# Scatters of the dense edges in node order, 108 of 508 of them and 75 dense blocks ahead of the first layer's pairs, and the gathers without their wait for dense progress

## What is computed

```python
def genconv(x, src, dst, W1, b1, g, be, W2, b2):          # three layers of the first network
    msg = relu(x[src]) + 1e-7
    m = segment_max(msg, dst)
    ex = exp(msg - m[dst])
    alpha = ex / segment_sum(ex, dst)[dst]
    out = segment_sum(msg * alpha, dst) + x               # per node: a softmax-weighted mean of its edges
    h = out @ W1 + b1
    h = relu((h - h.mean(0)) * rsqrt(h.var(0) + 1e-5) * g + be)
    return h @ W2 + b2

def layer(x, ea, src, dst, nw, ew, fnw, fnb, few, feb):   # three layers of the second network
    h, e = relu(x @ nw.T), relu(ea @ ew.T)
    n2 = relu(concat([segment_sum(e, dst), h]) @ fnw.T + fnb)
    e2 = relu(concat([h[src] + h[dst], e]) @ few.T + feb)
    return n2, e2

h = relu(layernorm(x)); x = x + three_genconv(h)          # relu behind each of the three
h = relu(layernorm(x)); x = x + three_layers(h, edge_attr)
```

## Time and profile before

| | |
|---|---|
| median of three runs | 4170.22 us (4170.03 to 4172.24) |
| the profiled execution | 4165.19 us, of which the span of the core is 4163.4 |
| mean granted clock of PE | 0.894 of full speed |
| PE busy | 3299.3 us, 79% |
| POOL busy | 2373.3 us, 57% |
| DVE busy | 2217.1 us, 53% |
| ACT busy | 1941.5 us, 47% |
| setup | 0 to about 863 us |
| first gather and last gather of layer 0 | 863.46 and 1391.62 us |

### The profile page before, as it was taken

How to read it: one execution, slowest core, us unless ns; L and a number is a source line. 1 busy time by engine, 2 the same in 40 slices (tenths; PEclk the granted TensorE clock), 3 DMA queues, 4 the chain that set the end, 5 groups by cost and what they waited for, 6 DMA issues and landing times.

```text
span 4163.4 us, 70803 instructions
## 1 busy us (share of the span) xinstructions
PE 3299.3 (79%) x19961; PEld 2595.9 (62%) x19961; DVE 2217.1 (53%) x5689; ACT 1941.5 (47%) x3697; POOL 2373.3 (57%) x2488
## 2 busy tenths in 40 slices
PE   2287777769898789888699888758788888888887
PEld 0144444458777677777577777746666666666665
DVE  6144333325444555445665445736666666666666
ACT  0222111146555576555585555734444444444444
POOL 2666666646666366666356665255565565565552
PEclk6588988889999899999899999879999999998988
DMA  7155433467777367777367776554444444444442
GB/s 291 54 184 191 138 119 120 124 202 246 248 235 236 117 231 234 251 234 242 110 230 243 243 235 197 151 160 126 124 129 129 127 128 128 128 125 127 127 125 63
DMA packets 419116, 713.14 MB, mean 171 GB/s; under 512 B 75585, under 2 KB 259067, under 8 KB 416098
## 3 DMA queue, kind: packets, MB, share of 16 engines
q0 software_dynamic: 130688, 321.08, 26.0%
q1 hardware_dynamic: 270119, 323.45, 25.5%
q10 hardware_dynamic: 18107, 66.24, 4.2%
HBM read 561.11 MB, written 149.39 MB: 171 GB/s over the span
## 4 chain that ended last, share of the span: by engine, by line
PE 36%; another core or an unknown queue 18%; issue 14%; DVE 14%; ACT 10%; DVEq 2%; ACTq 2%; DMA 1%; SPq 1%; POOL 0%; POOLq 0%
PE ps L1570 17%; PE ps L1593 4%; ACT casts L1466 2%; PE ps L718 2%; DVE acc L2369 2%; DVE acc L2403 2%; PE ps L2242 2%; DVE onehot L2396 1%; PE ps L2221 1%; ACTq L934 1%; DVE acc L2396 1%; PE ps L712 1%; ACT two_parts L1456 1%; PE ps L700 1%
## 5 line engine op out<-in xcount | busy, mean ns | idle before, releaser
L2211 POOL DMA_INDIRECT ring<-h_table,idx_ring x832 | 815.9, 981 | 563.2 <-issue 272.9
L652 POOL DMA_INDIRECT pair_rings<-split_table,src_idx x728 | 713.6, 980 | 409.8 <-issue 202.5
L1570 PE MATMUL ps<-casts,two_parts 128*128 128x500 f32 (+1 forms) x3464 | 823.1, 391 | 141.4 <-DVE two_parts L1660 73.8
L1570 PEld LDWEIGHTS ps<-casts,two_parts 128*128 128x128 f32 x3464 | 646.3, 198 | 280.2 <-DVE two_parts L1660 83.5
L665 POOL DMA_INDIRECT adjacency<-acc x508 | 495.8, 976 | 344.4 <-issue 144.7
L1660 DVE TENSOR_TENSOR two_parts<-work,two_parts 128x512 fp32r<-128x512 f32 (+1 forms) x276 | 187.4, 679 | 588.9 <-ACT two_parts L1456 349.8
L1466 ACT ACTIVATE casts<-spare 128x1000 fp32r<-128x1000 fp8e4 (+1 forms) x471 | 458.9, 974 | 8.5 <-PE ps L1570 4.8
L2308 ACT ACTIVATE work<-acc,vecs 128x512 f32<-128x512 f32 x208 | 150.2, 722 | 562.4 <-DVE acc L2369 303.5
L1456 ACT ACTIVATE two_parts<-work 128x512 fp32r<-128x512 f32 (+1 forms) x276 | 169.7, 615 | 452.8 <-remote 232.5
L2221 PE MATMUL ps<-ident,ring 128*128 128x128 f32 x1664 | 292.3, 298 | 83.6 <-issue 59.2
L2260 PEld LDWEIGHTS ps<-mats,work 128*128 128x128 f32 x1664 | 238.2, 204 | 141.7 <-issue 140.4
(11 more groups left out here) (333 smaller groups left out, 6242.6 us busy)
## 6 DMA issues: line engine op xcount, KB each, us to landing
spare<-adjacency SPq DMA_DIRECT2D x216, 250.0 KB
acc<-e_few SPq DMA_DIRECT2D x208, 256.0 KB
work<-msg_table SPq DMA_DIRECT2D x144, 256.0 KB
work<-in_edge_attr SPq DMA_DIRECT2D x104, 256.0 KB
e_few<-spare SPq DMA_DIRECT2D x52, 512.0 KB
spare<-rel_rows SPq DMA_DIRECT2D x208, 84.0 KB
spare<-adjacency SPq DMA_DIRECT2D x72, 187.5 KB
e_few<-work SPq DMA_DIRECT2D x26, 512.0 KB
```

Of the source, the lines that this page charges most:

```text
L652: e.indirect_dma_start(out=to, out_offset=None, in_=table, in_offset=bass.IndirectOffsetOnAxis(ap=src_idx[:, 2 * i + h, j:j + 1], axis=0)) ...
L1570: ins = e.matmul(bank, parts_of(d)[:, b % 2, q, kind * D:(kind + 1) * D], cast_counts[n % CASTS][:, at:at + width], start=opens, stop=(b = ...
L2211: e.indirect_dma_start(out=rows[:, s, j, :], out_offset=None, in_=h_table, in_offset=bass.IndirectOffsetOnAxis(ap=idx_ring[:, s, j:j + 1], ...
```

## The change

- **Order of the columns.** The 508 columns become 4 segments (SEGMENTS) of 127 (WIDE): row p of segment s holds 127 edges, and the segments lie behind one another in the order of destinations. Scatters 0 to 126 so fill the lowest destinations and 381 to 507 the highest. Each comparison on DVE covers 4 x (127 + k) columns instead of 508 + k, and a few small operations are added.
- **Clearing.** Regions 0 and 1 are cleared first; then x is loaded; then regions 2 and 3 are cleared. Scatter 0 waits for the first two regions alone, scatter 127 for the rest.
- **Where the scatters stand.** 400 (EARLY) stay in the setup, with their wait for the attributes; the last 108 stand on POOL at the head of the edges phase of layer 0, without that wait, ahead of the first gather. SP waits for all of them before it loads the first counts of region 2. The places and the counts get tiles of their own.
- **Dense blocks of layer 0.** 75 (LEAD_BLOCKS) stand in 15 steps ahead of the first pair, 5 in each; the other 121 are spread evenly over the 42 steps. Layers 1 and 2 keep their order.
- **Gathers.** The wait at h == 1 for `dense` is gone in all three layers; the wait for the sum of pair i-3 stays.

```diff
+SEGMENTS = 4
+WIDE = COLS // SEGMENTS
+REACH = WIDE + 2 * NEAR
+EARLY = 400
+LEAD = 15
+LEAD_BLOCKS = 75
...
-def step_of(n):
+def step_of(layer, n):
     r, b = divmod(n, BLOCKS)
+    columns = [sum(widths) for _, widths in REGIONS]
+    before = sum(BLOCKS * w for w in columns[0:r]) + b * columns[r]
+    if layer == 0:
+        lead = sum(columns[k // BLOCKS] for k in range(LEAD_BLOCKS))
+        if n < LEAD_BLOCKS:
+            return n * LEAD // LEAD_BLOCKS - LEAD
+        return (before - lead) * PAIRS // (BLOCKS * sum(columns) - lead)
...
             for h in range(2):
-                if h == 1:
-                    reached(e, S("dense"), blocks_halfway(i - 1))
...
-        def scatters(e, S):
-            e.wait_ge(S("zero_fill"), 16 * FILLS * len(REGIONS))
-            e.wait_ge(S("addresses"), 1)
-            for i in range(COLS):
+        def scatters(e, S, first, end):
+            for i in range(first, end):
                 n = i // EACH
+                if i == 0:
+                    e.wait_ge(S("zero_fill"), 16 * FILLS * 2)
+                if i == WIDE:
+                    e.wait_ge(S("zero_fill_rest"), 16 * (FILLS * (len(REGIONS) - 2) + 1))
                 if i % EACH == 0 and n >= SCATTERS:
                     e.wait_ge(S(f"gather_spread{n % SCATTERS}"), 16 * EACH * (n // SCATTERS))
-                if i % EACH == 0:
+                if i % EACH == 0 and i < EARLY:
                     reached(e, S("few_e0"), 2 * pairs_behind(n))
...
-                e.tensor_tensor(same[k % 4][:, 0:n], key[:, NEAR - k:NEAR + COLS], key[:, NEAR:NEAR + n], ALU.is_equal).then_inc(S("hit"), 1)
+                e.tensor_tensor(same[k % 4][:, :, 0:n], key[:, :, NEAR - k:NEAR + WIDE], key[:, :, NEAR:NEAR + n], ALU.is_equal).then_inc(S("hit"), 1)
...
-                scatters(e, S)
-                scattered(e, S)
+                e.wait_ge(S("addresses"), 1)
+                scatters(e, S, 0, EARLY)
+                scattered(e, S, EARLY)
                 split_stored0(e, S)
...
+                    for r in range(2):
+                        clear(r)
                 for k in range(5):
...
+                if not again:
+                    for r in range(2, len(REGIONS)):
+                        clear(r)
...
+                    if ready and d == 2 * DUOS:
+                        scattered(e, S, COLS)
...
             def pool(e, S):
+                if ready:
+                    scatters(e, S, EARLY, COLS)
                 for i in range(PAIRS):
                     reached(e, S("sums"), free_after(i))
...
-                for i in range(PAIRS + 3):
-                    blocks = [n for n in range(ALL_BLOCKS) if step_of(n) == i]
+                for i in range(-lead, PAIRS + 3):
+                    blocks = [n for n in range(ALL_BLOCKS) if step_of(layer, n) == i]
```

More of the change, by code:

```diff
@@ L83, in chunks_before @@
     return sum(len(widths) for _, widths in REGIONS[0:r])
-def step_of(n):
+def step_of(layer, n):
     r, b = divmod(n, BLOCKS)
+    columns = [sum(widths) for _, widths in REGIONS]
[5 more added lines that the diff above has]
+        return (before - lead) * PAIRS // (BLOCKS * sum(columns) - lead)
     if r == 0:
         return b * FIRST_STEPS // BLOCKS
[L91 to L99, removed]
+    first = BLOCKS * columns[0]
+    return FIRST_STEPS + (before - first) * (PAIRS - FIRST_STEPS) // (BLOCKS * sum(columns) - first)
 def slot_of(i):
@@ L140, in dense_jobs @@
             for n in range(width // CH):
-                jobs.append((step_of(BLOCKS * (r + 1) - 1) + 3, CUT + at + n * CH, chunks, False))
+                jobs.append((step_of(layer, BLOCKS * (r + 1) - 1) + 3, CUT + at + n * CH, chunks, False))
             at += width
-    out, now = [], -1
+    out, now = [], -LEAD - 1
     for ready, node, least, sparse in sorted(jobs):
@@ L922, in act, with clear @@
             def act(e, S):
+                def clear(r):
+                    width = PITCH if sum(REGIONS[r][1]) > PITCH // 8 * 7 else sum(REGIONS[r][1])
+                    rows = adjacency[r * SPAN * PITCH:r * SPAN * PITCH + NR * PITCH, :].rearrange("(p b d) o -> p b (d o)", b=BLOCKS, d=PITCH)
+                    for h in range(FILLS):
+                        at = slice(h * BLOCKS // FILLS, (h + 1) * BLOCKS // FILLS)
+                        n = at.stop - at.start
+                        zeros = Z0[:, 0:-(-n * width // 4)].bitcast(U8)[:, 0:n * width].rearrange("p (b d) -> p b d", d=width)
+                        e.dma_start(rows[:, at, 0:width], zeros).then_inc(S("zero_fill" if r < 2 else "zero_fill_rest"), 16)
                 if not again:
@@ L1295, in edges_phase @@
             columns = iota_w[:, :]
+            lead = LEAD if ready else 0
+            JOBS = JOBS_OF[layer]
             by_node = [work[0:WW, b, 0:2 * D] for b in range(2)]
@@ L1341, in duos_at @@
             def duos_at(i):
-                return [d for d in range(ALL_DUOS) if step_of(first_block(d)) == i + 1]
+                return [d for d in range(ALL_DUOS) if step_of(layer, first_block(d)) == i + 1]
             def blocks_of(u):
@@ L1355, in evacuated @@
             def evacuated(i):
[L1357 removed]
+                return [r for r in range(len(REGIONS)) if step_of(layer, BLOCKS * (r + 1) - 1) + 1 == i]
             def jobs_of(i):
@@ L1724, in dve @@
                     e.memset(hot_r[:, :, :, WW:P].bitcast(F32), 0.0).then_inc(S("blank"), 1)
-                for i in range(-1, PAIRS + 3):
+                for i in range(-lead - 1, PAIRS + 3):
                     if len(REGIONS) - 1 in evacuated(i):
```

102 lines of the change are left out of this document (51 added, 51 removed).

## The result

The changed kernel takes 4354.09 us (median of four runs, 4348.84 to 4369.62), the kernel before 4171.23 beside it: a ratio of 1.043 (95% interval 1.037 to 1.048), 183 us slower. The forecast was 4295 us with 4335 as its upper end. The direction was right, the size too small by 59 us. The profiled execution took 4348.84 us, its span 4347.1.

What follows compares the result with a forecast made beforehand. Limits differed by stage: scatters slowed the setup's loop, POOL and PE together set layer 0's pairs. Span 4163.4 + 125 (setup's 63 already taken off, layers 1 and 2 at 0) = 4288, median 4295 us; range 4150 to 4335.

Steps and rivals of the forecast that it cites:

- Start of the setup: Clearing half the table first lets scatter 0 start at 55 instead of 73.80: -18 us, bounds -12 and -20.
- End of the setup: Attributes' pairs speed up once 108 scatters leave: four at 6.10, 26 at 4.35, 137.5 instead of 182.9, -45 us.
- The crawl in the lead: Layer 0's head: unbroken indirect DMAs slow other engines to an instruction per 0.7 us or slower; PE does 15 blocks.
- until 967: Layer 0's head: POOL's 166 us stream ends at 967; PE then runs freely, 123 us to the first sum.
- Pairs of layer 0: Layer 0's pairs: 38 distances at 11.0 us, 418 us; the last gather starts at 1517.
- I take 11.0, between 10.3 and 11.7: Distance between layer 0's pairs, 11.66 before, POOL's least 10.0; the ends mean -27 and +27 us.
- The removed wait: Dropping the half-way wait in layers 1 and 2 was put at 0, with -88 and +15 kept.
- I take 0: Layers 1 and 2: no net gain, as longer streams bring the crawl; -88 if all pauses went, +15 otherwise.
- left as it was: What stands behind layer 0's last gather was assumed unchanged.
- the sign of the free lead: Layer 0's pair distance at which the freely overlapping lead turns from gain to loss, given as 10.4 us.
- The rival of a free lead: Layer 0's head: PE does 78 blocks beside POOL's stream, first sum at 981, median 4187; chance 0.22.

Runs made afterwards that it cites:

- e1: Changed kernel plus waits: every fourth of the 108 scatters heading layer 0 waits for PE's dense blocks to keep step; 4276.75 us, ratio 1.025.
- e11: Changed kernel with the last 108 scatters left out and 216 POOL fills in their place; 4238.5 us in one run.
- e17: Changed kernel where each 8th of the 108 scatters heading layer 0 waits until the last four have landed; 4252.11 us in one run, with the crawl.
- e16: Changed kernel itself, on a chip without the crawl; 3517.76 us against 3570.94 for the kernel before, ratio 0.985.
- e5: Kernel before with only node-order columns and two-part clearing, all 508 scatters in the setup, chip without the crawl; 3554.71 us, ratio 0.994.
- e4: Changed kernel with the gathers' wait for dense progress put back in all three layers; 4314.5 us, ratio 1.033.
- e18: Kernel before without the gathers' wait for dense progress, on a chip with the crawl; 4187.01 us, ratio 1.0023.
- e8: Changed kernel where each pair's third gather waits for the previous pair's gathers to land, chip without the crawl; 3591.31 us, ratio 1.006.
- e2: Changed kernel with all 508 scatters in the setup, the lead of dense blocks kept; 4282.89 us, ratio 1.026.
- e6: Kernel before without the gathers' wait for dense progress, on a chip without the crawl; ratio 0.9984.

## Why the prediction was right or wrong

**Start of the setup: right.** -18 forecast, first scatter at 55; it was 53.35, and the first store came 16.8 us earlier (187.16).

**End of the setup: right in kind, a little short.** 30 pairs in 784.73 - 659.47 = 125.3 us, 4.2 each from the first on, where I let four pass at 6.1 and gave 137.5: -12 us.

**The crawl in the lead: the mechanism right.** An unbroken stream, PE nearly still in its middle, then POOL idle for the first sum: all of it stands in the rows, and e1, e11 and e17 show that the stream of indirect DMAs makes it. PE did 16 blocks where I took 15, but that is luck: I let the crawl begin with PE's first block, at 9 us a block, while PE did 10 blocks nearly freely in its first 23 us and then 6 in the 121 until 957. The step that failed was "until 967", that the crawl ends with the stream. PE stood still for 17 us more, until 973.91. From there to the first sum it took 122 us for 62 blocks, jobs and a sum, as forecast for 63. The stream took 2.6 us more than 166, the wait behind it 16 more than 123: 19 us.

**Pairs of layer 0: wrong.** The step that failed was "I take 11.0, between 10.3 and 11.7". The distance was (1546.89 - 8.8 - 1096.20) / 38 = 11.63, as at the far end, +24 us. With less for PE to do it is still not POOL's 10 us that set the distance, but the crawl: POOL streams 8, 16 or 24 gathers and then pauses 1.8, 3.0 or 3.3 us. In the changed kernel, late in a stream of 24 (from 1223.53 to the pause before 1258.38), ACT, PE and POOL read:

```profile
1243.05 0.38 ACT L1522 ACTIVATE work<-ps 84x256 f32<-84x256 f32 x1 [11.42 <-remote]
...
1250.76 0.28 PE L1619 MATMUL ps<-end_rows,hot_r 128*128 128x256 f32 x1 [1.11 <-issue]
1252.17 0.37 PE L1619 MATMUL ps<-end_rows,hot_r 128*128 128x256 f32 x1 [1.13 <-issue]
...
1258.38 0.95 POOL L660 DMA_INDIRECT pair_rings<-split_table,src_idx  x1 [3.33 <-remote]
```

Part of a sum is done one matmul each 1.4 us, and POOL's pause follows. On the chip without the crawl the same kernel has 10.46 (e16). The 11.66 of before, too, was not what POOL and PE need, and it was one pair's: over 38 distances of layer 1 the kernel before has (1985.73 - 8.8 - 1503.78) / 38 = 12.45, and e5, without the crawl, 11.28. That breaks would shorten the pairs on a crawling chip is not shown.

**The removed wait: a term put at nothing.** The step that failed was "I take 0", with -88 and +15 as bounds: all that stands behind layer 0 lost 28 us together, the longer ways to the next layer more (+6, +6, +5) than the layers themselves (+7, +4). e4, which puts the wait back, gets 29 us back there, and e18, which only takes it out, loses 33. I had not looked at the ways at all, "left as it was". Why a way gets longer no run shows.

-12 + 19 + 24 + 28 = 59 us: the whole miss. One slip of the prediction's own: by its numbers the sign of the free lead turns at 10.6 us a pair, not 10.4, since 4187 - 4170 = 17 us over 38 distances are 0.4 below 11.0. The rival of a free lead was wrong for the chip of the result, and right for two others: with an unbroken stream of 82 scatters PE does 457 matmuls in 105 us in e8 as in e16. The ratio was 0.985 in e16, where I had written about no change, since I priced it with the setup of a crawling chip. And the Trainium skill's "A DMA cannot be slowed by a compute op, and vice versa" ("SBUF — State Buffer", section "SBUF: two separate sides"), which spoke for it, agrees with the rows of e16 (457 matmuls in 105 us beside 82 scatters), and not with those of 846 to 920 above (32 in 74 us beside 59). The sentence is about the ways into SBUF, and no run shows that the crawl arises there: the rows speak against what I took from it for the time.

## What to carry to other kernels

Before a step is hidden beside a long run of indirect DMAs, look in the trace for a stretch where such a run already stands, and read there what the other engines start, not how busy they are on average; where the crawl is, a break of the stream of some 3 us each 8 to 12 DMAs can be worth more than the time it takes (e17, e1). A queue that bounds the phase into which work is moved pays for it in full: here the 108 scatters cost POOL 136 us in layer 0 for 57 us at the setup's end (845.29 in e2 beside 788.39), unless, as on the chips of e16, they bounded the setup too. And a ratio from one chip is one chip's: run the kernel before beside the change on a second one before the change is kept or thrown away.

## What the runs showed of the hardware

- The same program took 4171 to 4180 us on three chips or more and 3571 to 3574 us on two, 17% apart, each within a per cent of itself. The difference stands in the stretches where POOL issues indirect DMAs without a break: the same setup has 36 matmuls in 75 us on one kind (e18) and 366 on the other (e6). The mean granted clock of the kernel before was 0.886 to 0.896 on the one and 0.933 to 0.939 on the other.
- With the crawl, the other engines go on for the first 14 to 48 us of an unbroken stream (14 in the setup; in the lead, where PE had stood idle before its first block, until about 836, 48 us behind 788.39), and then start an instruction each 0.7 to 1.4 us or stand still, for 11.42 us (ACT above) and up to 40 (PE in the lead, two blocks each 44.8 us), with the DMA engines at 6% of their time. It outlasts the stream: PE's next block came 17 us behind POOL's last DMA. Fills by POOL at 89% busy don't do it (e11). What in the stream does, the rows don't say, and no run here tells why two chips are free of it.
